# Two residual layers on one core: batch 0's h parts moved ahead of batch 1's weights on ScalarE and VectorE

## What is computed

```python
# layer 0
output = jnp.einsum('bsi,oi->bso', hidden_states, W) + b
sign = (2 * mask - 1).astype(hidden_states.dtype)
diff = jnp.einsum('bsi,bio->bso', hidden_states, sign)
x = x + output + diff * coeff[:, None, None]
# layer 1, A and Bm picked by the batch's slot, rank 16
base_out = jnp.einsum('bti,oi->bto', x, W) + b
lora_h = jnp.einsum('bti,bir->btr', x, A)
lora_out = jnp.einsum('btr,bro->bto', lora_h, Bm)
x = x + base_out + lora_out * SCALING
```

## Time and profile before

| what | before |
|---|---|
| runs, median of 3 | 384.35 us (383.54 to 384.43) |
| profiled execution, its own time | 382.39 us |
| its span | 380.4 us |
| TensorE busy (PE) | 369.7 us, 97% |
| VectorE busy (DVE) | 309.5 us, 81% |
| ScalarE busy (ACT) | 204.3 us, 54% |
| GpSimd busy (POOL) | 95.2 us, 25% |
| granted TensorE clock | 1.000 |
| chain that ended last | PE 90%, DMA 5%, POOL 2% |

### The profile page before, as it was taken

How to read it: one execution, slowest core, us unless ns; L and a number is a source line. 1 busy time by engine, 2 the same in 40 slices (tenths; PEclk the granted TensorE clock), 3 DMA queues, 4 the chain that set the end, 5 groups by cost and what they waited for, 6 DMA issues and landing times.

```text
span 380.4 us, 5424 instructions
## 1 busy us (share of the span) xinstructions
PE 369.7 (97%) x1934; PEld 311.9 (82%) x1934; DVE 309.5 (81%) x370; ACT 204.3 (54%) x314; POOL 95.2 (25%) x116
## 2 busy tenths in 40 slices
PE   7899997999999999999999999999999999999996
PEld 7788876888788887888788887888878887888875
DVE  4899989996899799985897869966899659987613
ACT  4546946385547476436652656525573366527520
POOL 1247391317004322033100450013300331002300
PEclk9999999999999999999999999999999999999999
DMA  7999995899619991499907995199924999073002
GB/s 273 410 399 379 325 387 207 271 375 386 246 50 270 390 386 66 120 320 396 326 0 232 354 380 196 47 252 386 387 89 120 315 386 339 2 239 141 0 0 110
DMA packets 45803, 94.73 MB, mean 249 GB/s; under 512 B 3514, under 2 KB 4562, under 8 KB 45778
## 3 DMA queue, kind: packets, MB, share of 16 engines
q1 hardware_dynamic: 42960, 85.73, 64.6%
q10 hardware_dynamic: 2754, 8.66, 5.7%
q0 software_dynamic: 64, 0.01, 0.0%
HBM read 86.00 MB, written 8.39 MB: 248 GB/s over the span
## 4 chain that ended last, share of the span: by engine, by line
PE 90%; DMA 5%; POOL 2%; issue 1%; DVE 1%; ACT 0%; SPq 0%; ACTq 0%; POOLq 0%
PE bank L534 42%; PE bank L503 27%; PE bank L509 14%; PE bank L545 4%; DMA ring_raw<-in_w 3%; PE bank L575 2%; DMA ring_raw<-in_mask 2%; POOL ring_raw L385 0%; POOL w_raw L396 0%; DVE w_two L977 0%; POOL b_parts L424 0%; PE bank L467 0%; POOL b_parts L422 0%; ACT w_two L674 0%; PE bank L477 0%
## 5 line engine op out<-in xcount | busy, mean ns | idle before, releaser
L534 PE MATMUL bank<-w_two,y_two 128*128 128x512 f32 x696 | 163.7, 390 | 0.7 <-DVE y_two L1026 0.7
L534 PEld LDWEIGHTS bank<-w_two,y_two 128*128 128x128 f32 x696 | 129.6, 188 | 28.5 <-DVE w_two L977 0.8
L667 ACT ACTIVATE ring<-ring_raw,coeff_neg 128x1024 fp32r<-128x1024 f32 (+1 forms) x67 | 74.5, 1114 | 112.6 <-DVE ring_raw L951 112.3
L503 PE MATMUL bank<-x_two,ring 128*128 128x512 f32 x448 | 126.8, 394 | 0.0
L951 DVE SCALAR_TENSOR_TENSOR ring_raw<-ring_raw,coeff_two 128x1024 f32<-128x1024 int32 (+1 forms) x67 | 83.3, 1256 | 16.7 <-DMA ring_raw<-in_mask 14.0
L961 DVE SCALAR_TENSOR_TENSOR ring<-ring_raw,coeff_neg,ring 128x1024 fp32r<-128x1024 f32 (+1 forms) x67 | 84.1, 1262 | 8.7 <-ACT ring L667 8.1
L390 POOL TENSOR_TENSOR ring_raw<-ring_raw,ident 128x128 f32<-128x128 f32 x56 | 39.3, 722 | 206.7 <-DMA ring_raw<-in_w 206.7
L503 PEld LDWEIGHTS bank<-x_two,ring 128*128 128x128 f32 x448 | 78.0, 189 | 11.6
L509 PE MATMUL bank<-x_two,ring 128*128 128x256 f32 x448 | 78.0, 281 | 0.0
L509 PEld LDWEIGHTS bank<-x_two,ring 128*128 128x128 f32 x448 | 70.6, 189 | 8.3
L1035 DVE TENSOR_TENSOR y_raw<-bank,y_raw 128x256 f32<-128x256 f32 x56 | 20.6, 420 | 22.1 <-ACT y_raw L705 22.1
(11 more groups left out here) (49 smaller groups left out, 213.2 us busy)
## 6 DMA issues: line engine op xcount, KB each, us to landing
ring_raw<-in_w SPq DMA_DIRECT2D x63, 512.0 KB, 8.5
ring_raw<-in_mask SPq DMA_DIRECT2D x63, 512.0 KB, 9.5
x_both<-in_x SPq DMA_DIRECT2D x31, 256.0 KB, 5.8
out<-z_rows ACTq DMA_DIRECT2D x15, 512.0 KB, 7.5
w_raw<-in_w SPq DMA_DIRECT2D x12, 512.0 KB, 12.2
b_raw<-in_lora_b SPq DMA_DIRECT2D x8, 448.0 KB, 3.7
ring_raw<-in_w SPq DMA_DIRECT2D x2, 256.0 KB, 4.2
ring_raw<-in_mask SPq DMA_DIRECT2D x2, 256.0 KB, 5.3
```

The costliest lines, as they stand in the source:

```text
L503: pe.matmul(layer0_bank(b, o)[:, 0:2 * T], w, x_two[:, k // PAIR, :, k % PAIR, :], start=(k == 0), stop=False, skip_group_check=True)
L534: ins = pe.matmul(bank[:], y_two[:, q, k, yp, :], w1_two[wp][:, j, k, :], start=(start and k == 0 and n == 0), stop=False, skip_group_chec ...
L667: act.activation(wc_hi[:, e % RING, lo:hi], sums[:, e % RING, lo:hi], ACT.Identity, bias=coeff_neg[:, b:b + 1]).then_inc(wc_hi_done, 1)
```

## The change

Four places change the order, and nothing else changes. On ScalarE, in batch 0, the high part of x's group 1 goes behind the two high parts of weight 1; and `h_high(0)` goes ahead of weight 1 of batch 1. On VectorE, in batch 0, the low part of x's group 1 goes behind the first low part of weight 1; and at the head of batch 1 the sums 0, 1 and 2 come first, with `h_low(0)` right behind them, and the low parts after it.

```diff
@@ ScalarE, batch 0
             for k in range(KT):
-                if k in (1, 3, 5):
+                if k in (3, 5):
                     x_high(0, (k + 1) // PAIR)
                 weights_high(0, k)
+                if k == 1:
+                    x_high(0, 1)
@@ ScalarE, batch 1
             weights_high(1, 0)
             lora_b_copy(0, 1)
+            h_high(0)
             weights_high(1, 1)
-            h_high(0)
             weights_high(1, 2)
@@ VectorE, batch 0
             weights_sum(0, 1, 1)
+            weights_low(0, 1, 0)
             x_low(0, 1)
-            weights_low(0, 1, 0)
             weights_sum(0, 2, 0)
@@ VectorE, batch 1
             x_low(1, 0)
+            weights_sum(1, 0)
             x_low(1, 1)
-            weights_sum(1, 0)
+            weights_sum(1, 1)
+            weights_sum(1, 2)
+            h_low(0)
+            weights_low(1, 0)
             x_low(1, 2)
+            weights_low(1, 1)
+            weights_sum(1, 3)
+            weights_low(1, 2)
             x_low(1, 3)
-            step(1, 0)
-            step(1, 1)
-            h_low(0)
-            step(1, 2)
             step(1, 3)
```

## The result

The changed kernel took 381.0 us (median of 6 executions, 380.74 to 382.0), the kernel before, run beside it, 384.08 (6 executions, 382.67 to 384.78): ratio 0.9936, 95% interval 0.9912 to 0.996. The change makes it 0.4 to 0.9% faster. The profiled execution of after took 380.74, span 378.8, which is 1.6 us less than that of before (382.39, span 380.4). So there are two parts to find: a profiled gain of 1.6 where 0.96 was worked out, and a gain between the medians, 3.1 here, that is larger still.

A forecast was written before the change was run, and what follows sets the result against it. The prediction took TensorE's 2.3 us wait at line 575 for h's low part as the bound: 0 + 2.33 - 1.37 = 0.96 us less, from 384.35 to 383.4 us, range 382.0 to 384.8.

The forecast's parts named there:

- The median of the runs is 1.96 above it: Final step: the profiled execution's 382.39 lies 1.96 under the median, so its 0.96 gain was taken from 384.35, giving 383.4.
- the term of VectorE behind line 987: VectorE after batch 1's diagonals: 0.29 us late throughout, so TensorE can be only 0.96 us early at weight 7's low part.
- rival 2: Weight 7 does not hold TensorE, as VectorE's rows shrink without GpSimd; all 2.33 us stays, 382.0 us; chance 0.10.
- the cap: At weight 7's low part in batch 1, TensorE can be at most 0.96 us early; the other 1.37 becomes waits.
- The bound and its release: Batch 0's closing products at line 575 wait 2.3 us for h's low part on VectorE; the whole 2.33 goes.
- Rival 3: Line 575's products are released by something else, or timed executions lack the stall: no gain, 384.3 us; chance 0.08.
- The price of the start: Edits in batch 0's weights: 0 us, between -0.1 and +0.1, for layer 1 of batch 0.
- The path of h: Batch 1's head: sum 0 at 51.46, h's high parts 57.37 to 58.52, low part 58.57, VectorE at the diagonals 71.11.
- Rival 1: GpSimd not brought forward, by the skill's rule; sum 0 stays at 52.06, gain 0.74, 383.6 to 383.8 us; chance 0.22.
- The waits that take the stall's place: TensorE's last two units before layer 1 of batch 1: 1.37 us of new waits, for weights 6 and 7.
- No loss behind it: After weight 7, at h's low part of batch 1 and later, nothing of the gain is lost.
- Rival 4: GpSimd starves in line 415, delaying h's low part to 59.8 to 61.4; up to 1.5 slower, 385.9 us; chance 0.08.

The follow-up runs named there:

- before_look3: The kernel before, unchanged, executed once more for another profile: 384.99 us, mean clock 0.996.
- filled_gap: Kernel before plus nine unread 512-column matmuls on TensorE ahead of batch 0's closing products: 382.55 us, ratio 0.9981.
- longer_gap_filled: Kernel before with h's low part behind step 2 on VectorE, plus twenty unread matmuls ahead of batch 0's closing products: 384.63 us, ratio 1.0036.
- longer_gap: Kernel before with h's low part moved behind step 2 on VectorE, lengthening the idle time before line 575: 387.5 us, ratio 1.0107.
- before_again: The kernel before, unchanged, run again for its scatter and a second profile: 383.28 us, ratio 0.9998.
- before_look: The kernel before, unchanged, executed once more for another profile: 382.47 us, full clock.
- before_look2: The kernel before, unchanged, executed once more for another profile: 382.82 us, full clock.
- h_only: Kernel before with only batch 1's edits (h's high part earlier on ScalarE, VectorE's new order), batch 0's weights as before: 381.17 us, ratio 0.9951.
- x1_ahead: Changed kernel with VectorE's low part of x group 1 again ahead of sum 0 in batch 1: 380.99 us, one execution.
- vector_only: Changed kernel with h's high part on ScalarE again behind weight 1's in batch 1: 382.05 us, one execution.
- start_only: Kernel before with only the two edits in batch 0's weights, batch 1 as before: 383.71 us, ratio 1.0013.
- w22_on_pool: Changed kernel with line 987's four diagonal rows done by GpSimd instead of VectorE: 381.28 us, ratio 0.9949.

## Why the prediction was wrong, and what of it was right

**What failed first: "The median of the runs is 1.96 above it, their spread 0.9, so the same difference is taken from 384.35".** The difference between the profiled execution and the median was carried over as if it were a constant of measuring; in the changed kernel it is 0.26 (381.0 and 380.74). 1.4 to 1.6 of the 1.96 was the cost of the very wait that the change removes: 40 of 78 executions have the lower mean clock, and the one of them that has a profile shows it falling right behind that wait. The profiled execution had a clock of 1.00 throughout, so no row of it shows this; what could have been seen is that its 382.39 lay 1.15 below the lowest of the three times. The Trainium skill, page "TensorE: Matmul & The Clock Gate", Part 1, says that a TensorE that has been idle is put back to half rate. before_look3's 0.50 behind 2.40 us of idle time agrees. The run filled_gap, which keeps the wait and fills the idle time, and longer_gap_filled, 2.9 us faster than longer_gap, show that it is the idleness and not the lateness. This part was not on the list of rivals: none of them lets a wait cost more than its length. With this step alone put right, the profiled 382.39 - 0.96 and the 0.26 above it would have given 381.7.

**What failed second, in the term of VectorE behind line 987: "From 70.82 on VectorE's order is the old one, without idle time, so all of it is 0.29 late".** VectorE came to line 987 at 71.11, as worked out, but weight 7's low part ended at 82.44 (81.16 + 1.28), 0.22 *before* the old 82.66 instead of 0.29 after. The order was the old one, its durations were not. VectorE's two pairs of diagonals took 0.75 and 0.48 us, where before they took 1.02 each. The kernel before had GpSimd's diagonals of line 390 beside both of them (GpSimd's timeline of before):

```profile
70.48 1.21 POOL L390 TENSOR_TENSOR ring_raw<-ring_raw,ident 128x128 f32<-128x128 f32 x2 [12.11 <-DMA ring_raw<-in_w]
...
74.35 1.99 POOL L390 TENSOR_TENSOR ring_raw<-ring_raw,ident 128x128 f32<-128x128 f32 x2 [2.66 <-DMA ring_raw<-in_w]
```

In after they run from 67.99 to 73.58, 2.5 us ahead like TensorE, whose units free the ring places for their transfers, and are over when VectorE comes to the second pair. A row of line 987 takes 0.24 us by itself (0.48 for two) and up to 0.5 beside GpSimd (1.02 for two in before, 0.75 in after's first pair). From start to next start the two pairs cost 0.82 less than before (0.78 and 0.52 for 1.06 each), the two sums of line 1011 that now stand beside GpSimd 0.30 more (1.37 us each for 1.22), and the net 0.51 is what VectorE made up. This is rival 2's mechanism ("because VectorE's rows of 70 to 83 shrink without GpSimd beside them"), held against by "they run at their normal 1.2 each already": that is true of the large rows, and the small ones were left out of it. With it the cap is 0.96 + 0.51 = 1.47, which is what TensorE was early at weight 7's low part (82.49 against 83.96); at layer 1 it was 1.37 (84.48 against 85.85), and in stretch 1, 1.34, counted from batch 0's low rank product, which was itself 0.08 early. The missing 0.3 to the span's 1.6 is the start and the scatter named above.

That GpSimd's rows are the cause shows in the kernel before itself. In before_look3 they come later and clear of both pairs (VectorE and GpSimd):

```profile
71.08 0.48 DVE L985 TENSOR_TENSOR w_raw<-w_raw,ident 128x128 f32<-128x128 f32 x2
75.86 0.49 DVE L985 TENSOR_TENSOR w_raw<-w_raw,ident 128x128 f32<-128x128 f32 x2
72.43 2.12 POOL L390 TENSOR_TENSOR ring_raw<-ring_raw,ident 128x128 f32<-128x128 f32 x2 [13.79 <-DMA ring_raw<-in_w]
76.62 2.71 POOL L390 TENSOR_TENSOR ring_raw<-ring_raw,ident 128x128 f32<-128x128 f32 x2 [2.07 <-DMA ring_raw<-in_w]
```

Both pairs are short, with VectorE's order unchanged. In longer_gap_filled the pair at 70.41 is clear of GpSimd's 72.47 and takes 0.49, and the pair at 75.46 stands beside its 75.31 and takes 1.02. The pairs of before_again, before_look and before_look2 took 1.02 and 0.75, 0.76 and 1.02, 1.02 and 0.75. So the profile that the forecast stepped through happened to be the dearest, and part of the 0.51 is the meeting of two executions: in h_only, x1_ahead and vector_only the pairs took 1.01 or 1.02 and 0.48 or 0.49, and stretch 1 is 40.30 to 40.33 instead of 40.16.

**What was right.**
- The bound and its release. The products at line 575 stood for h's low part alone; with it at 58.47 they don't wait. Rival 3 fell.
- The price of the start, by the ratio: start_only's 1.0013, an interval that holds no change. The forecast's -0.1 to +0.1 us for layer 1 of batch 0 held in after's profile (36.06) but not in others with the same edits (up to 36.84).
- The path of h: sum 0 at 51.44 for 51.46, h's high parts 57.27 to 58.44 for 57.37 to 58.52, h's low part 58.47 for 58.57, VectorE at the diagonals at 71.11 for 71.11 (to the hundredth by luck: it was 0.10 ahead at 58.92, and the row beside GpSimd's 67.99 took 0.10 more). Rival 1, with sum 0 at 52.06, fell: line 406 ended 0.45 us behind VectorE's pause in both orders (x1_ahead, 4.68 us), which the rule cited there would not have. But x1_ahead also shows that this advance was not needed.
- The waits that take the stall's place: 1.3 us of gaps before 78.78, 81.25 and 82.49, forecast 1.37. The size of these waits came out right because the stall was larger than read (2.50 for 2.33, by the overlap of modelled ends) while VectorE was also earlier.
- No loss behind it: stretch 2 was 47.06 and 47.07. h's low part of batch 1 ran at 101.25 for a product at 102.71.
- Rival 4, GpSimd starved in line 415, fell: those rows got through.

**What stays open.** Why the clock falls in one execution and not in the next behind the same 2.4 us was not found. Nor was it traced why VectorE comes to batch 2's low part of h later in one execution than in the next, which makes the scatter of up to 1 us in the stretch behind stretch 2.

## What to carry to other kernels

Before a difference between a profiled execution and the median is carried over, list each execution's granted clock and span: a stall that costs TensorE its clock in some executions costs more in the median than a profile at full clock shows, and removing it, or filling it with matmuls that nobody reads, gives that back too. When an engine that others wait for is put earlier, transfers and GpSimd's work move with it, so the durations of VectorE's rows must be read again with their neighbours, the small ones included. And a stall that is removed entirely is seldom a gain of its length: here 1.3 of 2.5 us came back 20 us later, and pulling on that point made the next batch's closing product wait.

## What the runs showed of the hardware that was not expected

- Behind an idle time of 2.40 us on a TensorE otherwise busy one profile shows half clock for 3.4 us; 40 of 78 executions of the same program have the mean clock that goes with it, at a cost of 1.4 to 1.6 us. With 4.77 us of idle time it is 4 of 4, and 6.8 us in the profile.
- Nine matmuls of 512 columns in that idle time kept the clock in 12 of 12 executions, twenty in the longer one in 10 of 10.
- VectorE's 128x128 additions cost up to twice as much beside GpSimd's (0.5 for 0.24 us), its 128x1024 rows 1.48 for 1.28. GpSimd's 128x128 additions took 5.01 us for four beside VectorE in w22_on_pool, and 0.88 for two at their shortest (after, at 80.43).
